# GpSimd's residual-and-bias sum and mask conversion wait for VectorE's second normalised rows

## The chip, the core and the metric

The kernel runs on one core of a Trainium2 chip. A core has TensorE (PE in the profile), VectorE (DVE), ScalarE (ACT), GpSimd (POOL) and SyncE (SP); each takes its own instructions in program order and meets the others only through semaphores. The metric is the time on the device in microseconds (us), as the median of several runs.

## What is computed

Two layers over `x` of shape (16, 256, 256): 16 entries of 256 tokens by 256 features. The first layer (conditioned normalisation, a router, eight experts) takes about the first 630 us and is not touched. The second is a transformer layer, cut here to what matters:

```python
x = _ln(src) * (1.0 + scale) + shift
q = (x @ Wq + bq); k = (x @ Wk + bk); v = (x @ Wv + bv)       # 16 heads of 16
scores = q @ k.T / 4 + attention_bias                          # (16, 16, 256, 256)
scores = where(src_mask, -inf, scores)
ctx = softmax(scores) @ v
x = x + (ctx @ Wo + bo)                                        # first residual
h = _ln(x) * g2 + beta2                                        # second normalisation
ff = _gelu2(h @ W1 + b1) @ W2 + b2
return x + ff                                                  # second residual
```

## The kernel before

**Staging.** `step(n, par)` is written once for each engine and called for n = -2 to 17. Step n holds the attention of entry n, and beside it the projections of entry n+1 and the end of entry n-1 (output projection, second normalisation, feed-forward). n = 3 to 12 are a hardware loop, two steps to a turn; the rest are unrolled. Within a step, PE, DVE and ACT go through 16 heads h and take up the other entries' work at fixed heads, so the order on each engine is written by hand. "An entry" below is one such step.

**Attention of one head.** PE `scores` (L1349, L1351) fills a PSUM bank from the mask and from q and k; DVE `minimum` (L1586, a custom instruction and an accumulator read for each of two halves) adds the bias and takes the row minimum; ACT `exponentials` (L1254) writes the probabilities over the bias; PE `turn_probs` (L1363) transposes them; ACT or DVE `take_probT` (L1260, L1592) brings them back to SBUF; PE `weigh` (L1379) multiplies by the values. `scores` and `turn_probs` alternate between two banks each, so PE's scores of head h+2 wait for the minimum of head h.

**The end of entry n-1, in step n.** DVE at h = 4: `residual` (L1633) writes `x3`, the first residual, and `moments` (L1639 to L1645) its mean and variance. GpSimd: `rsqrt` (L1180) turns the variance into `rstd2`. DVE at h = 5: `normalise2` writes the normalised rows `h_rows`, two instructions (one for each 128 tokens) of 128 x 256 float32, each with a mean and an inverse deviation per partition, each adding 1 to `h_rows_ready`:

```python
for j in range(J):
    dve.tensor_scalar(h_rows[:, j, :], x3[:, j, :], mv2[:, j, 0:1], rstd2[:, j:j + 1],
                      ALU.subtract, ALU.mult).then_inc(sem("h_rows_ready"), 1)
```

Right behind it DVE has `take_values` for entry n+1 (L1624, `v_pad`), the minimum of head 7 and `split_hT` (L1656). PE at h = 6 transposes `h_rows` (`turn_h`, L1448), ACT at h = 6 rounds the result (`take_hT`, L1289, `hT_hi`) and PE at h = 7 starts the feed-forward (`feed_up`, L1463). In the profile's tile names trailing numbers are cut, so `x3` is written x, `rstd2` rstd, `mv2` mv.

**GpSimd in step n.** Its queue holds: the gather for entry n+2 (L1185 to L1191); `rsqrt` of entry n-1; `prepare_sum` of entry n-1 (L1210: `x3b` = `x3` + `b2`, 128 x 512 float32, which only `finish` at h = 15 reads); `take_mask` of entry n+1 (L1205: the mask bytes become float32, first read by PE's scores at h = 14); four `lower_gelu` (L1198, `act_lo`); `rsqrt` of entry n+2.

**The xn rows.** `normalise` (L1576) at h = 14 is the same instruction as `normalise2` on other tiles (`src` to `xn`). `combine_second` (L1558) adds gathered rows to `src`, with both of its tensor inputs in SBUF.

Of the kernel before, what the change touches and what calls it, by code (L numbers as in the profile page):

```python
# [18 lines left out]
J = T // P  # L19
# [42 lines left out]
def wait_alone(eng, sem, value):  # L62


    if isinstance(value, int):
        eng.wait_ge(sem, value)
    else:
        value = eng.to_reg(value)
        eng.wait_ge(sem, 1)
        eng.wait_ge(sem, value)  # L70


def wait_free(eng, sem, value, alone=False):

    if isinstance(value, int):
        if value > 0:
            eng.wait_ge(sem, value)
    elif alone:
        wait_alone(eng, sem, value)
    else:  # L80
        eng.wait_ge(sem, value)


def exists(n):

    return not isinstance(n, int) or 0 <= n < B
# [8 lines left out]
def entries(eng, step):  # L95


    for n in range(-2, 3):
        step(n, n % 2)
    with eng.Fori(1, B // 2 - 2) as i:  # L100
        step(2 * i + 1, 1)
        step(2 * i + 2, 0)
    for n in range(B - 3, B + 2):
        step(n, n % 2)


def spread(ap, shape, at):

    return ap.unsqueeze(at).to_broadcast(shape)
# [874 lines left out]
def transformer(nc, ctx, io, keep):  # L984
# [3 lines left out]
    def sem(name):  # L988
        if name not in sems:
            sems[name] = ctx.enter_context(nc.semaphore(name))  # L990
        return sems[name]
# [181 lines left out]
    @block.gpsimd  # L1173
    def _(pool):
        pool.memset(minus_half[:], -0.5).then_inc(sem("half_set2"), 1)
        pool.wait_ge(sem("half_set2"), 1)

        def rsqrt(out, var, ready, done, n):
            pool.wait_ge(sem(ready), n + 1)
            pool.tensor_tensor(out[:], var[:, :, 1], minus_half[:], ALU.pow).then_inc(sem(done), 1)  # L1180

        def gather(n):
            wait_free(pool, sem("src_read"), n)
            wait_free(pool, sem("xmT_ready"), C * n)
            pool.tensor_copy(gate_now[:], gates[:, bass.ds(n, 1), :, :].rearrange("p b k j -> p (b k j)")).then_inc(sem("entry_cols"), 1)  # L1185
            pool.tensor_copy(mod_now[:, 0, :], scale[:, :, bass.ds(n, 1)].rearrange("p c b -> p (c b)")).then_inc(sem("entry_cols"), 1)
            pool.tensor_copy(mod_now[:, 1, :], shift[:, :, bass.ds(n, 1)].rearrange("p c b -> p (c b)")).then_inc(sem("entry_cols"), 1)
            pool.tensor_copy(row_now[:], out_row[:, bass.ds(n, 1), :].rearrange("p b q -> p (b q)")).then_inc(sem("entry_cols"), 1)
            wait_alone(pool, sem("entry_cols"), 4 * (n + 1))
            for q in range(K * J):  # L1190
                pool.indirect_dma_start(picked_rows[:, q, :], None, io["expert_out"],  # L1191
                                        bass.IndirectOffsetOnAxis(ap=row_now[:, q:q + 1], axis=0),
                                        bounds_check=TILES * TOK - 1, oob_is_err=False).then_inc(sem("rows_in"), 16)

        def lower_gelu(n, pair):
            wait_alone(pool, sem("act_upper"), 4 * n + pair + 1)
            at = 2 * pair % 4
            pool.tensor_tensor(act_part["lo"][:, 2 * pair:2 * pair + 2, :], up_f[:, at:at + 2, :],  # L1198
                               act_part["hi"][:, 2 * pair:2 * pair + 2, :].bitcast(F32), ALU.subtract).then_inc(sem("act_split"), 1)

        def take_mask(n, par):
            wait_alone(pool, sem("mask_in"), 16 * (n + 1))
            if at_least(n, 2):
                wait_alone(pool, sem("scores_done"), H * (n - 1))
            pool.tensor_scalar(mask_f[par][:], mask[:].bitcast(U8), 1.0, None, ALU.mult).then_inc(sem("mask_taken"), 1)  # L1205

        def prepare_sum(n):
            pool.wait_ge(sem("x3_ready"), n + 1)
            wait_free(pool, sem("out_sent"), 16 * n)
            pool.tensor_tensor(x3b[:], x3[:], spread(b2[:], [P, J, D], 1), ALU.add).then_inc(sem("x3b_ready"), 1)  # L1210

        def step(n, par):
            if exists(n + 2):
                gather(n + 2)
            if exists(n - 1):
                rsqrt(rstd2, mv2, "var2_ready", "rstd2_ready", n - 1)
                prepare_sum(n - 1)
            if exists(n + 1):
                take_mask(n + 1, 1 - par)
            if exists(n - 1):  # L1220
                for pair in range(4):
                    lower_gelu(n - 1, pair)
            if exists(n + 2):
                rsqrt(rstd, mv, "var_ready", "rstd_ready", n + 2)

        entries(pool, step)

    @block.scalar
# [572 lines left out]
def at_least(n, least):  # L1801

    return not isinstance(n, int) or n >= least
# [88 lines left out]
```

## Time and profile before

| | |
|---|---|
| median of 3 runs | 1423.8 us (1423.69 to 1425.08) |
| the profiled execution: time, span | 1427.18 us, 1425.4 us |
| busy over the span: PE, DVE, ACT, POOL | 1276.8, 988.0, 903.1, 665.1 us |
| granted TensorE clock, mean | 0.976 of full speed |
| one entry of the transformer, steady part | about 46 us |

The span runs from the first to the last instruction of the profiled execution. Busy time of an engine is an average over stages with different limits; what a change does is read from the waits of the stage in which it lies.

### The profile page before, as it was taken

Reading aid. Unit: us, or ns where it says so; the run is one execution under the profiler, and the core shown is the slowest. Engines: PE = TensorE matmul, PEld = TensorE weight load, DVE = VectorE, ACT = ScalarE, POOL = GpSimd, SP = SyncE. Lnnn points to the kernel's source line nnn. Section 1 sums busy time; section 2 is a strip of 40 time slices with the busy share of each in tenths; the row PEclk is TensorE's granted clock in tenths of the full one; section 3 lists DMA queues with packets and bytes.
Section 4 is the critical chain, followed back from the end, with each engine's and each line's share of the span. In section 5 each row is a group of like instructions: output and inputs, shape, how many; then the busy total and the mean of one; then the engine's idle time right before and its main releaser. Section 6 shows DMA issues by size and latency. Waiting matters only on the chain. (4 is left out here: it accounts for less than half of the span.)

```text
span 1425.4 us, 34480 instructions
## 1 busy us (share of the span) xinstructions
PE 1276.8 (90%) x9923; PEld 1160.8 (81%) x9923; DVE 988.0 (69%) x2764; ACT 903.1 (63%) x2319; POOL 665.1 (47%) x580
## 2 busy tenths in 40 slices
PE   5884899999999999945899999999999999999996
PEld 4774899999999999944587888778877878788885
DVE  5776688889878987743776667566766667666652
ACT  3442677778777877722566676666666666667671
POOL 2775577787778777743032332332232232231221
PEclk9999999999999999976899999999999999999997
DMA  5885121121112111128766656655675556654620
GB/s 189 271 274 187 46 66 46 57 61 51 57 48 65 54 56 58 49 89 253 225 214 184 190 182 198 205 181 162 195 220 182 177 179 204 199 189 148 202 72 15
DMA packets 184707, 203.18 MB, mean 143 GB/s; under 512 B 18176, under 2 KB 172736, under 8 KB 184576
## 3 DMA queue, kind: packets, MB, share of 16 engines
q1 hardware_dynamic: 169136, 161.57, 36.9%
q10 hardware_dynamic: 9264, 23.47, 5.1%
q0 software_dynamic: 6176, 16.79, 3.4%
q14 instruction: 96, 0.79, 0.2%
q8 instruction: 35, 0.57, 0.2%
HBM read 155.89 MB, written 41.68 MB: 139 GB/s over the span
## 5 line engine op out<-in xcount | busy, mean ns | idle before, releaser
L1254 ACT ACTIVATE bias<-bias,neg_max 128x256 f32<-128x256 f32 x512 | 255.4, 501 | 193.7 <-DVE neg_max L1586 191.6
L343 POOL TENSOR_TENSOR w_lo<-w,w_hi 128x512 fp32r<-128x512 f32 x156 | 242.2, 1572 | 0.0
L1586 DVE CUSTOM_DVE_ANT_0 bias<-ps_s,bias 128x256 f32<-128x256 f32 x512 | 194.5, 417 | 34.0 <-PE ps_s L1351 21.4
L745 DVE TENSOR_TENSOR w_lo<-w,w_hi 128x512 fp32r<-128x512 f32 x156 | 149.8, 999 | 68.7 <-ACT w_hi L423 67.0
L544 PE MATMUL ps_y<-w_hi,hidT_hi 128*128 128x256 f32 x624 | 180.2, 289 | 1.9 <-DVE token_rows L759 1.9
L531 PE MATMUL ps_h<-htokT_hi,w_hi 128*128 128x256 f32 x624 | 178.5, 286 | 3.2 <-DVE htokT_lo L750 3.2
L531 PE MATMUL ps_h<-htokT_lo,w_hi 128*128 128x256 f32 x624 | 178.2, 286 | 0.0
L531 PE MATMUL ps_h<-htokT_hi,w_lo 128*128 128x256 f32 x624 | 178.1, 285 | 0.0
L1349 PE MATMUL ps_s<-mask_f,minus_ident 128*128 128x256 f32 x512 | 154.3, 323 | 25.6 <-DVE neg_max L1586 15.8
L544 PE MATMUL ps_y<-w_lo,hidT_hi 128*128 128x256 f32 x624 | 177.0, 284 | 0.0
L544 PE MATMUL ps_y<-w_hi,hidT_lo 128*128 128x256 f32 x624 | 177.0, 284 | 0.0
L1198 POOL TENSOR_TENSOR act_lo<-up_f,act_hi 128x512 fp32r<-128x512 f32 x64 | 82.6, 1291 | 198.1 <-ACT act_hi L1301 198.1
L1363 PE MATMUL ps_p<-const,bias 128*128 128x128 f32 x1024 | 158.7, 278 | 16.9 <-ACT bias L1254 15.6
L1349 PEld LDWEIGHTS ps_s<-mask_f,minus_ident 128*128 128x128 f32 x512 | 97.9, 191 | 59.1 <-DVE neg_max L1586 39.5
L1180 POOL TENSOR_TENSOR rstd<-mv,minus_half 128x2 f32<-128x2 f32 x32 | 23.2, 724 | 254.4 <-DVE mv L1645 179.9
L1363 PEld LDWEIGHTS ps_p<-const,bias 128*128 128x128 f32 x1024 | 116.6, 141 | 29.3 <-issue 17.9
L1351 PE MATMUL ps_s<-k_stack,q_stack 128*128 128x256 f32 x512 | 134.2, 284 | 0.0
L531 PEld LDWEIGHTS ps_h<-htokT_hi,w_hi 128*128 128x128 f32 x624 | 121.5, 195 | 3.9 <-DVE htokT_lo L750 3.9
L544 PEld LDWEIGHTS ps_y<-w_hi,hidT_hi 128*128 128x128 f32 x624 | 120.0, 192 | 2.1 <-DVE token_rows L759 2.1
L531 PEld LDWEIGHTS ps_h<-htokT_lo,w_hi 128*128 128x128 f32 x624 | 121.5, 195 | 0.0
L531 PEld LDWEIGHTS ps_h<-htokT_hi,w_lo 128*128 128x128 f32 x624 | 121.4, 195 | 0.0
L544 PEld LDWEIGHTS ps_y<-w_lo,hidT_hi 128*128 128x128 f32 x624 | 120.3, 193 | 0.0
(276 smaller groups left out, 3496.9 us busy)
## 6 DMA issues: line engine op xcount, KB each, us to landing
bias<-bias_dram SPq DMA_DIRECT2D x128, 512.0 KB, 4.2
w<-w_dram ACTq DMA_DIRECT2D x32, 512.0 KB
xin<-dispatch SPq DMA_DIRECT2D x39, 256.0 KB, 2.8
expert_out<-token_rows SPq DMA_DIRECT2D x39, 256.0 KB, 2.2
q_stack<-q_hi_rows SPq DMA_DIRECT2D x64, 128.0 KB, 2.9
q_stack<-q_lo_rows SPq DMA_DIRECT2D x64, 128.0 KB, 2.9
k_stack<-k_hi_rows SPq DMA_DIRECT2D x60, 128.0 KB, 2.8
k_stack<-k_lo_rows SPq DMA_DIRECT2D x60, 128.0 KB, 2.8
```

The costliest lines, as they stand in the source:

```text
L343: pool.tensor_tensor(w2_part["lo"][:, k, :], w2_piece(e, k), w2_part["hi"][:, k, :].bitcast(F32), ALU.subtract).then_inc(sem("w2_split"), 1)
L531: last = pe.matmul(ps_h[f // 2][:, (f % 2) * TOK:(f % 2 + 1) * TOK], w1_part[a][:, C * (f // 4) + c, (f % 4) * P:(f % 4 + 1) * P], htokT[b ...
L544: last = pe.matmul(ps_y[j][:, 0:D], hidT[a][:, f, j * P:(j + 1) * P], w2_part[b][:, k, (f % 2) * D:(f % 2 + 1) * D], start=(f == 0 and n = ...
L745: dve.tensor_tensor(w1_part["lo"][:, k, :], w1_piece(e, k), w1_part["hi"][:, k, :].bitcast(F32), ALU.subtract).then_inc(sem("w1_split"), 1)
L1180: pool.tensor_tensor(out[:], var[:, :, 1], minus_half[:], ALU.pow).then_inc(sem(done), 1)
L1198: pool.tensor_tensor(act_part["lo"][:, 2 * pair:2 * pair + 2, :], up_f[:, at:at + 2, :], act_part["hi"][:, 2 * pair:2 * pair + 2, :].bitca ...
L1254: act.activation(head_rows(h, j), head_rows(h, j), ACT.Exp, scale=-1.0, bias=neg_max[par][:, h, j:j + 1], accum_out=total[par][:, h, j:j + ...
L1349: pe.matmul(ps_s[h % 2][:, j * T:(j + 1) * T], minus_ident[:], mask_f[par][:, j, :], start=True, stop=False)
L1351: last = pe.matmul(ps_s[h % 2][:, j * T:(j + 1) * T], q_stack[par][:, h, j * P:(j + 1) * P].bitcast(F32R), k_stack[par][:, h // 2, :].bitc ...
L1363: last = pe.transpose(ps_p[h % 2][:, kt * T + j * P:kt * T + (j + 1) * P], head_rows(h, j)[:, kt * P:(kt + 1) * P], ident)
L1586: dve.tensor_tensor_reduce(head_rows(h, j), ps_s[h % 2][:, j * T:(j + 1) * T], head_rows(h, j), -1.0, LARGEST, ALU.add, ALU.min, neg_max[p ...
```

## The change

One wait is added on GpSimd, ahead of `prepare_sum`. `J` is 2 and `h_rows_ready` counts two per entry, so `J * n` is reached when both instructions of `normalise2` for entry n-1 have written. `take_mask` and all that follows stand behind it in the same queue.

```diff
             if exists(n - 1):
                 rsqrt(rstd2, mv2, "var2_ready", "rstd2_ready", n - 1)
+                pool.wait_ge(sem("h_rows_ready"), J * n)
                 prepare_sum(n - 1)
             if exists(n + 1):
                 take_mask(n + 1, 1 - par)
```

On GpSimd, in the even step of the hardware loop, the rows read as follows (`x3b<-x,b` is the sum, `mask_f<-mask` the conversion; REGISTER_ALU rows work out a semaphore's value):

```order
 L1179 REGISTER_ALU
 L1180 TENSOR_TENSOR rstd<-mv,minus_half 128x2 [waits var2_ready]
-L1210 TENSOR_TENSOR x3b<-x,b 128x512 [waits out_sent,x3_ready]
+L1217 REGISTER_ALU
+L1210 TENSOR_TENSOR x3b<-x,b 128x512 [waits out_sent,x3_ready,h_rows_ready]
 L68 REGISTER_ALU
 L68 REGISTER_ALU [waits mask_in]
```

No instruction changes its place; the sum gets one more semaphore to wait for, and a register instruction that works out `J * n`.

On DVE, at heads 5 to 6 of a step in the same loop, the rows are these before the change, and the same after it (the ISA rows of L1586 are the minimum of a head, `v_pad<-ps_q,bv` is `take_values`):

```order
L1586 ISA bias,neg_max<-ps_s,bias 128x256
L1586 ISA neg_max 128x1
L1651 TENSOR_SCALAR h_rows<-x,mv,rstd 128x256 [waits h_turned,rstd2_ready]
L1651 TENSOR_SCALAR h_rows<-x,mv,rstd 128x256
L1624 TENSOR_TENSOR v_pad<-ps_q,bv 128x4x4x16 [waits pv_done,v_done]
L1624 TENSOR_TENSOR v_pad<-ps_q,bv 128x4x4x16
L68 REGISTER_ALU
L1586 ISA bias,neg_max<-ps_s,bias 128x256 [waits scores_done]
L1586 ISA neg_max 128x1
```

Nothing moved here: the `h_rows` pair still waits for `rstd2` and still stands ahead of the values and of the minimum of head 7; what is new is that GpSimd's sum starts behind the pair instead of beside it.

## Rows read from the trace of the kernel before

**Rows 1.** One entry's stretch: length, busy us by engine, clock, DMA
```profile
core 0: us, PE busy (x) PEld busy (x) DVE busy (x) ACT busy (x) POOL busy (x), PEclk, DMA share, GB/s
754.00:799.70 45.70, 43.02 (x352) 36.99 (x352) 30.55 (x106) 30.33 (x94) 14.08 (x16) 1.00 0.63 193
```

**Rows 2.** Timeline, one entry, heads 4 to 8: start, length, engine, idle before
```profile
769.52 1.89 PE L1438 MATMUL ps_q<-wv,xmT 128*128 128x256 f32 x8
...
771.61 0.28 PE L1351 MATMUL ps_s<-k_stack,q_stack 128*128 128x256 f32 x1
...
773.06 1.27 POOL L1210 TENSOR_TENSOR x3b<-x,b 128x512 f32<-128x512 f32 x1
773.11 2.00 DVE L1651 TENSOR_SCALAR h_rows<-x,mv,rstd 128x256 f32<-128x256 f32 x2
...
774.17 0.65 PE L1363 MATMUL ps_p<-const,bias 128*128 128x128 f32 x4 [0.17 <-ACT bias L1254]
774.32 1.53 POOL L1205 TENSOR_SCALAR mask_f<-mask 128x512 fp32r<-128x512 uint8 x1
...
775.03 0.74 DVE L1624 TENSOR_TENSOR v_pad<-ps_q,bv 128x256 f32<-128x256 f32 x2
...
775.16 0.66 PE L1448 MATMUL ps_k<-const,h_rows 128*128 128x128 f32 x4 [0.34 <-DVE h_rows L1651]
...
776.49 0.51 ACT L1254 ACTIVATE bias<-bias,neg_max 128x256 f32<-128x256 f32 x1 [1.89 <-DVE neg_max L1586]
...
776.51 0.39 PE L1349 MATMUL ps_s<-mask_f,minus_ident 128*128 128x256 f32 x1 [0.69 <-DVE neg_max L1586]
...
777.63 0.66 PE L1363 MATMUL ps_p<-const,bias 128*128 128x128 f32 x4 [0.38 <-ACT bias L1254]
777.96 0.58 ACT L1289 ACTIVATE hT_hi<-ps_k 128x512 fp32r<-128x512 f32 x1
...
778.58 0.69 DVE L1656 SCALAR_TENSOR_TENSOR hT_lo<-ps_k,hT_hi 128x512 fp32r<-128x512 f32 x1 [2.12 <-ACT hT_hi L1289]
...
778.60 0.38 PE L1463 MATMUL ps_q<-hT_hi,ff_hi 128*128 128x256 f32 x1 [0.31 <-ACT hT_hi L1289]
```

**Rows 3.** Timeline of DVE: TENSOR_SCALAR from SBUF to SBUF with GpSimd idle
```profile
682.19 0.60 DVE L1685 TENSOR_SCALAR h_rows<-const,vec 128x128 f32<-128x128 f32 x2
...
796.83 0.74 DVE L1576 TENSOR_SCALAR xn<-src,mv,rstd 128x256 f32<-128x256 f32 x2 [0.16 <-POOL rstd L1180]
```

**Rows 4.** Timeline: DVE beside GpSimd's act_lo, and (698.23) with GpSimd idle
```profile
698.23 0.88 DVE L1552 SCALAR_TENSOR_TENSOR src<-picked_rows,gate_now,x 128x256 f32<-128x256 f32 x2
...
783.86 1.29 POOL L1198 TENSOR_TENSOR act_lo<-up_f,act_hi 128x512 fp32r<-128x512 f32 x1 [8.02 <-ACT act_hi L1301]
...
784.77 0.68 DVE L1664 SCALAR_TENSOR_TENSOR up_f<-tanh_f,ps_k 128x512 f32<-128x512 f32 x1
...
792.18 1.29 POOL L1198 TENSOR_TENSOR act_lo<-up_f,act_hi 128x512 fp32r<-128x512 f32 x1 [1.17 <-ACT act_hi L1301]
792.31 1.85 DVE L1558 SCALAR_TENSOR_TENSOR src<-picked_rows,gate_now,src 128x256 f32<-128x256 f32 x2
```

**Rows 5.** Instructions of L1586: duration ns min/median/max, first and last start
```profile
L1586 DVE CUSTOM_DVE_ANT_0 bias<-ps_s,bias x512: 401/418/426, 665.1 to 1385.2; 128x256 f32<-128x256 f32 x171
```

**Rows 6.** Timeline: the pair in the last two entries
```profile
1364.63 1.68 DVE L1651 TENSOR_SCALAR h_rows<-x,mv,rstd 128x256 f32<-128x256 f32 x2
...
1403.24 1.67 DVE L1651 TENSOR_SCALAR h_rows<-x,mv,rstd 128x256 f32<-128x256 f32 x2 [0.82 <-POOL rstd L1180]
```

**Rows 7.** Timeline of a loop entry: SP's bias load, DVE's minimum of head 14
```profile
923.01 1.10 SPq L1106 DMA_DIRECT2D bias<-bias_dram  x2
...
932.17 0.41 DVE L1586 CUSTOM_DVE_ANT_0 bias<-ps_s,bias 128x256 f32<-128x256 f32 x1
```

**Rows 8.** DMA issues of 891 to 940 us: KB each, median us to landing
```profile
bias<-bias_dram SPq DMA_DIRECT2D x9, 512.0 KB, 3.9
```

**Rows 9.** Timeline: PE's first scores of the next entry
```profile
797.06 0.39 PE L1349 MATMUL ps_s<-mask_f,minus_ident 128*128 128x256 f32 x1
```

## The prediction

> **What bounds the kernel now.** The change touches only the transformer, so I began with the busy table by stretches. In the steady part an entry takes 45.7 us, of which PE is busy 43.0, DVE and ACT 30 to 31, at full granted clock and with the DMA engines busy 0.63 of the time [rows 1]. PE sets the pace but stands still 2.7 us per entry, and only a change that removes part of this shortens an entry. The timeline of one entry shows where: around heads 6 and 7, PE waits 0.34 us for `h_rows`, 0.69 for a minimum, 0.38 for exponentials and 0.31 for `hT_hi`, 1.72 us in a row [rows 2]. All four follow from one lateness on DVE. Its two `h_rows` instructions start at 773.11 and take 2.00 us; then come, without a gap, the values and the minimum of head 7, whose end releases both ACT, at 776.49, after a wait of 1.89 us, and PE's next scores; and on ACT the exponentials of head 7 stand ahead of `hT_hi`, which releases DVE's `hT_lo` (waited 2.12 us) and PE's feed-forward [rows 2].
>
> The pair need not take 2.00 us. The same instruction on `xn`, same shape and same kind of scalars, takes 0.74 us for two with GpSimd idle [rows 3]. What differs is that GpSimd's sum starts 0.05 us ahead of the pair and runs 1.27 us, and the mask conversion follows at 774.32 [rows 2]. Two independent rows bear out that DVE is held there: a pair of scalar-tensor-tensor instructions with both tensors in SBUF takes 0.88 us with GpSimd idle and 1.85 when GpSimd's `act_lo` starts 0.13 us ahead of it [rows 4]; and in the last two entries, where the pair has the sum beside it but no mask conversion, it takes 1.68 and 1.67 us [rows 6].
>
> **What the change does, part by part.** GpSimd's sum now starts when both `h_rows` instructions have written.
>
> *The pair on DVE.* It starts as before, since `rstd2` comes before the wait. With nothing beside it I take 0.74 us, by the `xn` row. It saves 2.00 - 0.74 = 1.26 us in the entry shown; the other 13 entries with a mask conversion read 1.97 to 2.00, mostly 1.99, so 1.25 each. In the last two, 1.68 - 0.74 and 1.67 - 0.74, 0.94 and 0.93.
>
> *How much of it reaches the end of the entry.* DVE: the values were multiplied by 769.52 + 1.89 = 771.41 and the scores of head 7 were done at 771.89, so values and minimum follow at once and ACT is released at 775.23, not 776.49; it had waited 1.89 us, more than 1.26, so its exponentials come the full 1.26 earlier. PE: the transposition of `h_rows` can start only when the head before is done, at 774.82, so it ends at 775.48 (775.82 before, 0.34 gained). The scores then start at 775.48, 1.03 earlier, and end by about 776.2; the next transposition waits for ACT, at 777.63 - 1.26 = 776.37, so these scores are hidden. `hT_hi` starts on ACT at 776.70, when the transposed rows have lain there 1.2 us, and PE's feed-forward at 777.34 instead of 778.60. DVE's `hT_lo` waited 2.12 us and moves with it [rows 2]. From there all four engines stand 1.26 us earlier, and I count the whole of it.
>
> *What doesn't move with them.* SP's transfers start from earlier work. The nearest: the bias of heads 14 and 15 is issued at 923.01 [rows 7], lands in 3.9 us [rows 8], 926.9, and is read at 932.17 [rows 7]. That leaves 5.3 us, after the change about 4.0, so it costs nothing.
>
> *The two GpSimd instructions.* Sum and conversion start about 0.8 us later (773.85 for 773.06) and end near 776.7. Behind them in the queue stand `act_lo`, which waited 8.02 us [rows 4] and keeps over 6 of that, and, on SP, the next mask load, a step away. The mask is first read at 797.06 [rows 9], `x3b` only at the end of the step. All cost nothing; were the cover gone, the price would be the 0.8 us. The register instruction and the wait lie in the same idle time.
>
> *What the sum now lies beside.* This the trace does not show: 1.27 us of sum beside DVE's values and the minimum of head 7, both with PSUM as one input. Bounds: at best nothing (the values already take 0.74 us beside the conversion [rows 2], so there is hardly anything to gain either); at worst what `act_lo` did to the pair with two SBUF tensors, 1.85 - 0.88 = 0.97 us. I take nothing: the nearest rows are `up_f` (one SBUF input, one PSUM input), 0.68 us and begun while `act_lo` ran [rows 4], and the minimum, which over 512 runs never took more than 426 ns against a median of 418 [rows 5].
>
> The Trainium skill says on this case, in "SBUF — State Buffer", section "Who interferes with whom", that a VectorE instruction with at most one SBUF input outside the two-port modes does not contend with GpSimd; that would make the cost nothing too, for the sum as for the conversion.
>
> *Weighed against a rule.* The conversion beside the second `h_rows` instruction seems to cost little: the pair is 0.32 us longer with it than without (2.00 against 1.68) [rows 2, 6]. The same section of the Trainium skill says that between a two-port VectorE instruction and GpSimd whoever comes second is blocked until the other has finished. For the first instruction the trace agrees, since the pair cannot have ended before the sum did. For the second it does not: held for the whole conversion, to 774.32 + 1.53 = 775.85, the pair would have taken 3.0 us and more, and the row has 2.00. By that rule a saving reckoned from it would be some 2.3 us an entry, 35 in all; the measured length decides, and it gives 1.25.
>
> **Sum.** 14 x 1.25 + 0.94 + 0.93 = 19.4 us. The profiled execution had a span of 1425.4 and a time of 1427.2; the span becomes 1406.0. The median of the runs shown is 1423.8, 3.4 below that execution's time; less the same 19.4 it is 1404.4.
>
> **The rivals.**
> *1. Part of it is absorbed.* If after the transposition something other than DVE set PE's pace, each entry would give only PE's wait for `h_rows`, 0.34 us [rows 2], in the last entry all 0.93: 15 x 0.34 + 0.93 = 6.0 us, 1417.8. For it: PE is the busiest engine, and its scores at 775.48 gain only 1.03. Against: every later wait in the row names DVE or ACT work behind the pair. Chance 0.07, anywhere between.
>
> *2. No change, because `h_rows` is not slowed by GpSimd.* The price is then nothing, 1423.8. That would follow if the instruction used one SBUF input at one element a cycle. A row speaks against it: two of 128 x 128 take 0.60 us and two of 128 x 256 take 0.74 [rows 3], 0.14 us for 256 elements, while from PSUM 256 elements more cost 0.68 - 0.42 = 0.26 us [rows 4, 5]. The instruction runs at the double rate. Nor does anything but GpSimd explain 0.74 against 2.00. The case that the wait does nothing, because its count is reached too early, belongs here; the count is two per entry, so it does not. Chance 0.05.
> The Trainium skill ("SBUF — State Buffer", "Who interferes with whom") counts `tensor_scalar` in that double rate among those that contend, so it sides with the forecast.
>
> *3. Slower, because the hold moves.* Sum and conversion, 1.27 + 1.53 = 2.80 us from 773.85, now lie beside the values, the minimum of head 7 and the start of the chain to `hT_hi`. If DVE were held for all of it, an entry would lose 2.80 - 1.26 = 1.54 us; over 14 entries 21.6 us longer, 1445, less what the last two give. It decides from 1.26 us of stretch per entry. Against: the values beside the conversion are already seen unslowed, and so are `up_f` and the minimum. Chance 0.04, with smaller stretches in the forecast's range.
>
> **How the numbers follow.** The forecast has 0.84, and its own range is 1402 to 1409: below, a little more than the sum if runs scatter as before; above, 0.3 us per entry lost at PE or beside the sum. To hold 8 in 10 with the upper half of that and some of rival 1, I give 1402 to 1411. A measurement of this kernel tells about 0.2%, 2.8 us, from no change. Faster: the forecast and nearly all of rival 1, 0.90. Within 0.2%: rival 2 and the weakest end of rival 1, 0.06. Slower: 0.04.
>
> **What would show it.** In the changed kernel's timeline `h_rows` x2 reads 0.74 us in all 16 entries and GpSimd's sum starts as it ends. `v_pad` x2 stays at 0.74 and the minimum under 0.43. PE's waits at the transposition and the scores behind it nearly vanish, and an entry takes 44.4 to 44.7 us with PE still busy 43.0. The pair still near 2 us would show rival 2; the pair at 0.74 with `v_pad` or the minimum stretched, rival 3; all of these as forecast and an entry still above 45.1 us, rival 1, and then the wait that has grown names the cause. The forecast also fails if SP's transfers come late: DVE's minimum would then wait for a bias DMA.

## The result, and the profile after

| | before | after |
|---|---|---|
| median | 1424.44 us (4 runs, 1423.69 to 1425.38) | 1401.63 us (4 runs, 1397.94 to 1403.61) |
| ratio, 95% interval | | 0.9837 [0.9817, 0.9857] |
| profiled execution: time, span | 1427.18, 1425.4 us | 1400.47, 1398.7 us |
| granted TensorE clock, mean | 0.976 | 0.978 |

The kernel is 22.8 us faster. The forecast was 19.4 us, from 1423.8 (the median of three of the four runs before) to 1404.4, with a range from 1402.0: the result lies 2.8 us below the forecast and 0.4 below the range. The direction, the place and the mechanism came as written; the size is short, and most of what follows is about the 3.4 us by which the gain exceeds 19.4.

The timeline of the changed kernel at the same heads of the same entry, which answers to [rows 2] (`...` stands for lines left out):

```profile
768.99 0.74 DVE L1652 TENSOR_SCALAR h_rows<-x,mv,rstd 128x256 f32<-128x256 f32 x2
...
769.64 0.75 DVE L1625 TENSOR_TENSOR v_pad<-ps_q,bv 128x256 f32<-128x256 f32 x2
769.80 1.28 POOL L1210 TENSOR_TENSOR x3b<-x,b 128x512 f32<-128x512 f32 x1 [0.85 <-DVE h_rows L1652]
...
770.05 0.66 PE L1364 MATMUL ps_p<-const,bias 128*128 128x128 f32 x4 [0.18 <-ACT bias L1255]
...
770.54 0.60 PE L1449 MATMUL ps_k<-const,h_rows 128*128 128x128 f32 x4
...
771.05 1.50 POOL L1205 TENSOR_SCALAR mask_f<-mask 128x512 fp32r<-128x512 uint8 x1
771.11 0.51 ACT L1255 ACTIVATE bias<-bias,neg_max 128x256 f32<-128x256 f32 x1 [0.63 <-DVE neg_max L1587]
771.13 0.39 PE L1350 MATMUL ps_s<-mask_f,minus_ident 128*128 128x256 f32 x1
...
772.25 0.66 PE L1364 MATMUL ps_p<-const,bias 128*128 128x128 f32 x4 [0.38 <-ACT bias L1255]
772.58 0.58 ACT L1290 ACTIVATE hT_hi<-ps_k 128x512 fp32r<-128x512 f32 x1
...
773.20 0.69 DVE L1657 SCALAR_TENSOR_TENSOR hT_lo<-ps_k,hT_hi 128x512 fp32r<-128x512 f32 x1 [2.12 <-ACT hT_hi L1290]
773.22 0.39 PE L1464 MATMUL ps_q<-hT_hi,ff_hi 128*128 128x256 f32 x1 [0.31 <-ACT hT_hi L1290]
```

The pair takes 0.74 us for 2.00, the sum now names `h_rows` as what it waited for, `v_pad` keeps its length beside the sum, and PE's waits of 0.34 and 0.69 are gone while those of 0.38 and 0.31 stay. From the start of the pair to `hT_lo` it is 773.20 - 768.99 = 4.21 us, and in [rows 2] 778.58 - 773.11 = 5.47: the forecast's 1.26 us, to the hundredth.

All 32 instructions of the pair, the sum, and the minimum (duration in ns, min/median/max), the last for [rows 5]:

```profile
L1652 DVE TENSOR_SCALAR h_rows<-x,mv,rstd x32: 407/411/415, 725.3 to 1377.8; 128x256 f32<-128x256 f32 x32
L1210 POOL TENSOR_TENSOR x3b<-x,b x16: 1263/1278/1281, 726.1 to 1378.3; 128x512 f32<-128x512 f32 x16
L1587 DVE CUSTOM_DVE_ANT_0 bias<-ps_s,bias x512: 402/419/426, 664.6 to 1360.3; 128x256 f32<-128x256 f32 x171
```

The steady part by windows. Its first row is the entry of [rows 1], the second the 14 entries from the first `h_rows` pair to the 15th, the third the rest of the span:

```profile
core 0: us, PE busy (x) PEld busy (x) DVE busy (x) ACT busy (x) POOL busy (x), PEclk, DMA share, GB/s
749.70:793.60 43.90, 42.88 (x354) 37.23 (x353) 29.49 (x107) 30.40 (x94) 14.07 (x16) 1.00 0.63 200
725.30:1340.72 615.42, 591.75 (x4878) 513.01 (x4873) 405.85 (x1469) 422.54 (x1283) 186.98 (x207) 1.00 0.62 195
1340.72:1398.70 57.98, 46.21 (x350) 40.81 (x350) 22.22 (x69) 24.54 (x67) 13.59 (x11) 0.90 0.09 28
```

The same two stretches of the profile before, and PE's waits in ten entries of each kernel (us in total, times, longest), before first:

```profile
727.44:1364.63 637.19, 597.16 (x4881) 512.76 (x4873) 423.36 (x1469) 423.27 (x1283) 186.89 (x208) 1.00 0.61 188
1364.63:1425.40 60.77, 47.66 (x350) 41.64 (x350) 24.10 (x69) 24.57 (x67) 13.46 (x11) 0.88 0.08 27
```

```profile
PE ps_p L1363 <- ACT bias L1254: 10.1, 30, 0.4
PE ps_s L1349 <- DVE neg_max L1586: 7.8, 10, 0.8
PE ps_out L1420 <- DVE ctxT L1611: 4.6, 9, 0.5
```

```profile
PE ps_p L1364 <- ACT bias L1255: 10.3, 32, 0.4
PE ps_q L1464 <- ACT hT_hi L1290: 2.4, 10, 0.3
PE ps_out L1421 <- DVE ctxT L1612: 2.1, 4, 0.5
```

The 14 entries give 637.19 - 615.42 = 21.8 us, where the pair accounts for 14 x 1.25 = 17.5; the rest of the span behind them gives 2.8, for 1.87. Ahead of the first pair, where the change can do nothing, since the new wait first holds back the sum that used to lie beside that pair, it is 727.44 - 725.30 = 2.1 us. PE's wait for the minimum, 7.8 us, has left the list, which is the change. Its wait for `ctxT` (the result of the attention, transposed for the output projection) has halved too, though nothing near it was touched. These differences ask whether the profile before was typical.

### The profile page after: what moved, and what is told of

Same layout as the page of the kernel before. It is cut to its first block and busy times, and to the rows that moved or that the text cites. A ratio compares the mean times of both kernels' runs of the same rounds, so it can differ in the third digit from the quotient of the medians.

```text
span 1398.7 us, 34496 instructions
## 1 busy us (share of the span) xinstructions
PE 1266.9 (91%) x9923; PEld 1157.5 (83%) x9923; DVE 968.6 (69%) x2764; ACT 902.8 (65%) x2319; POOL 665.3 (48%) x580
```

## The experiments

Eleven runs on three chips of this kind; each set of repeats has its own runs of the kernel before on the same chip, and gains are reckoned from those.

**1. Both kernels again (e1, e2).** No edit.

> The kernel before, unchanged, run again. The hold on the h_rows pair must be there in the same size: 1.97 to 2.00 us in 14 entries, 1.67 and 1.68 in the last two. It is run for the surplus of the change over the forecast, which in the two profiles lies between finish and the ctxT product of the next step (heads 0 to 2): ACT starts the copy of head 2 late by 0.36 to 0.62 us in 9 entries of the kernel before, in none of the first 14 of the changed one. If that is a property of this kernel's timing, it shows here again in the same entries. If it belongs to one execution, it is gone or in other entries. Time: 1423 to 1427 us, ratio 1.000 in either case.

> The changed kernel, run again with more rounds, to size the gain. If the forecast's sum of 19.4 us was the whole of it and the rest was scatter of single executions (the four runs so far lie 5.7 us apart), the ratio is 0.9864 or nearer to 1. If the late copy of head 2 on ACT, 0.5 us in 8 or 9 entries, is really gone as well, 19.4 + 4.5 = 23.9 us go and the ratio is 0.983. The pair stays at 0.74 us, v_pad x2 at 0.74 to 0.75.

Measured: before 1425.0 us (1423.36 to 1426.97, 12 runs) and 1424.16 (17 more); after 1401.68 (1398.36 to 1402.91, 5 runs), ratio 0.9834 [0.9817, 0.985]. A gain of 22.5 us on this chip shows that the surplus over 19.4 isn't chance. In the profile of e1 PE's waits over the 14 entries, and under it the same row of e11 (below), the same kernel on another chip:

```profile
PE ps_out L1420 <- DVE ctxT L1611: 3.0, 5, 0.8
```

```profile
PE ps_out L1420 <- DVE ctxT L1611: 6.1, 13, 0.8
```

The wait for `ctxT` differs for one and the same kernel. Over all profiles the step on VectorE from `q_lo` (the low part of the projected queries) to `ctxT` reads 3.54 us in e1 to e4, 3.96 to 4.47 in eight of the entries of e5 to e8, and 3.8 to 4.2 in the same ones of e9 to e11, whichever kernel ran: among these three chips it goes by the chip. The profile before has 4.02 to 4.28 there, the one after 3.53 to 3.54, so 4.5 us of the 26.7 between their spans is no effect of the change. Nor are the 2.1 us ahead of the first pair: over the 13 profiles that pair starts at 725.3 to 729.6 us, whichever kernel ran. That leaves 20.1 us between the two profiles, for 19.4. The ratio of e2 is the one that its expectation gave for the late copy gone as well, but not for that reason, since on this chip the step is 3.54 us in both kernels. Why the medians differ by 22.5, and the two dips of the clock that e1 shows besides, come under 6.

**2. The conversion beside the pair (e3).**

```diff
                 rsqrt(rstd2, mv2, "var2_ready", "rstd2_ready", n - 1)
-                pool.wait_ge(sem("h_rows_ready"), J * n)
-                prepare_sum(n - 1)
             if exists(n + 1):
                 take_mask(n + 1, 1 - par)
+            if exists(n - 1):
+                pool.wait_ge(sem("h_rows_ready"), J * n)
+                prepare_sum(n - 1)
```

> GpSimd converts the mask right after the reciprocal root, beside the h_rows pair, and takes the sum only when the pair has written. If every GpSimd instruction holds the pair for its whole length, the first h_rows row waits for the conversion's end and the pair takes 1.53 + 0.70 = 2.2 us in 14 entries, so that all of the gain there is gone and a little more (14 x 0.2 = 3 us slower than before). If the conversion, which read only bytes and cost the second row 0.32 us, holds less, the pair takes 1.1 to 1.5 us and about half of the gain stays (10 us faster than before). In the last two entries there is no conversion and the pair takes 0.74 us in either case.

Measured: 1405.63 us (4 runs, 1405.57 to 1406.96), ratio 0.9872 [0.9855, 0.989], 3.95 above e2. One entry, and all instructions of the pair:

```profile
772.67 1.54 POOL L1205 TENSOR_SCALAR mask_f<-mask 128x512 fp32r<-128x512 uint8 x1
772.70 1.04 DVE L1653 TENSOR_SCALAR h_rows<-x,mv,rstd 128x256 f32<-128x256 f32 x2
```

```profile
L1653 DVE TENSOR_SCALAR h_rows<-x,mv,rstd x32: 399/410/721, 728.7 to 1383.6; 128x256 f32<-128x256 f32 x32
```

A conversion that starts 0.03 us ahead and runs 1.54 costs the pair 0.30 us, all in its first instruction (0.72 for 0.41); the second runs beside it at full speed. 14 x 0.30 = 4.2 us, and 3.95 were measured. The pair of 1.04 us is shorter than in either case of the expectation (1.1 to 1.5, or 2.2).

**3. The sum far away (e4).** The wait stays, with the conversion behind it; the sum goes behind the second `act_lo`.

```diff
                 pool.wait_ge(sem("h_rows_ready"), J * n)
-                prepare_sum(n - 1)
...
                 for pair in range(4):
                     lower_gelu(n - 1, pair)
+                    if pair == 1:
+                        prepare_sum(n - 1)
```

> As the changed kernel, but the sum comes between the second and the third act_lo, where GpSimd was idle 2.25 us, and only the mask conversion follows the pair. Beside the values and the minimum of head 7 there is then the conversion instead of the sum. If the sum costs nothing there, as forecast, v_pad x2 and the minimum read the same as in the changed kernel and the time is the same within 0.2%. If the sum did stretch them, this kernel is faster than the changed one by 14 times the stretch. The sum in the gap meets only PSUM-fed work on DVE; should it push act_lo later, feed-forward waits and it is slower by up to 0.3 us per entry, 4.8 us.

Measured: 1403.14 us (4 runs, 1402.33 to 1404.38), ratio 0.9853 [0.9835, 0.987]; `v_pad` 0.75, the minimum 0.42, the pair to `hT_lo` 4.20 to 4.21, all as in the changed kernel. The sum beside `v_pad` and the minimum costs nothing: there was nothing to win back.

**4. What of GpSimd's work holds the pair (e6, e7).** In e6 the sum waits for the first row only. In e7, on the kernel before, the instruction beside the pair has one input; `b2` is left out.

```diff
-                pool.wait_ge(sem("h_rows_ready"), J * n)
+                pool.wait_ge(sem("h_rows_ready"), J * n - 1)
```

```diff
-            pool.wait_ge(sem("x3_ready"), n + 1)
-            wait_free(pool, sem("out_sent"), 16 * n)
-            pool.tensor_tensor(x3b[:], x3[:], spread(b2[:], [P, J, D], 1), ALU.add)
+            wait_alone(pool, sem("x3_ready"), n + 1)
+            wait_free(pool, sem("out_sent"), 16 * n, alone=True)
+            pool.tensor_scalar(x3b[:], x3[:], 1.0, None, ALU.mult)
```

> The changed kernel, but GpSimd waits for the first h_rows instruction only, so that the sum starts about 0.1 us after the second one has begun. Theory 1 (VectorE gives way whenever GpSimd's sum runs): the second instruction takes about as long as the sum, 1.27 us and a bit, the pair 0.41 + 1.38 = 1.8 us with only 0.2 us saved against before, and the time is 1424.2 - 14 x 0.2 = 1421. Theory 2 (whoever starts second waits): the second row has begun already and takes 0.41, the sum waits for it and reads 1.3 to 1.6 us; the pair is 0.74 to 0.8 and the time that of the changed kernel, 1401.7. A pair of 1.2 to 1.5 us (1411 to 1416) would be neither: both slowed while they overlap.

> The kernel before, but GpSimd's instruction beside the pair multiplies x3 by 1.0 instead of adding b2 to it (the bias b2 is left out of the computation): one float32 tensor read instead of two, same output, same place; its waits stand in instructions ahead of it. Theory 1 (it is the two float32 inputs that hold VectorE; the conversion with its one input costs the pair 0.30 us): the first row takes 0.4 to 0.7, the pair 1.0 to 1.4 us with both GpSimd instructions beside it, and the time is 1424.2 - 14 x 0.8 - 2 x 0.6 = 1411.8, between 1408 and 1416. Theory 2 (any float32 instruction of GpSimd between SBUF tiles holds it): first row 1.38, pair 1.7 to 2.0, time 1422 to 1425.

Measured: e6 1406.18 us (4 runs, 1405.12 to 1408.12), ratio 0.9855 [0.984, 0.987]; e7 1411.12 (4 runs, 1410.48 to 1412.37), ratio 0.9892 [0.9877, 0.9908]. The kernel before took 1426.01 on this chip, 1.8 more than the expectations reckoned with. For e7 the pair's lengths give 14 x 0.95 + 2 x 0.64 = 14.6 us, and 14.9 were measured. First e6, then e7:

```profile
862.14 0.74 DVE L1652 TENSOR_SCALAR h_rows<-x,mv,rstd 128x256 f32<-128x256 f32 x2
...
862.63 1.39 POOL L1210 TENSOR_TENSOR x3b<-x,b 128x512 f32<-128x512 f32 x1 [0.53 <-DVE h_rows L1652]
```

```profile
771.17 1.54 POOL L1210 TENSOR_SCALAR x3b<-x 128x512 f32<-128x512 f32 x1
771.21 1.04 DVE L1651 TENSOR_SCALAR h_rows<-x,mv,rstd 128x256 f32<-128x256 f32 x2
```

In e6 the second row had begun when the sum came: the row keeps its 0.41, and the sum reads 1.38 (median) for 1.28, though in the entry shown 0.25 us of the row were still to come. In the kernel before, the sum came 0.05 us ahead, and the first row took up to 1.38. The one that starts second is the one that loses. The Trainium skill says so in "SBUF — State Buffer", section "Who interferes with whom": "Issue order, not op shape, decides who blocks." Here the traces agree for the sum, in both orders. The same section of the Trainium skill says that the other is held for the whole instruction. The traces bear this out only for VectorE behind the sum: e7's float32 instruction with one input starts 0.04 us ahead, runs 1.54, and costs the pair 0.30, as the byte conversion did. So the GpSimd instruction with two tensor inputs holds VectorE through, and the two with one only at their start. Whether it is the second input or the kind of instruction (TENSOR_TENSOR or TENSOR_SCALAR) that decides, e7 doesn't tell, since it changed both. The 2.00 us of [rows 2] come apart as 0.74 + 0.97 for the sum + 0.30 for the start of the conversion.

**5. The other collision (e8).** The additions of gathered rows, which read 0.99 and 1.85 us beside `act_lo`, move on VectorE to head 3, before `k_lo`.

```diff
+                if exists(n + 2) and not (isinstance(n, int) and n == -1) and h == 3:
+                    combine_first(n + 2)
+                    combine_second(n + 2)
...
-                    if h == 11:
-                        combine_first(n + 2)
-                    if h == 12:
-                        combine_second(n + 2)
```

> The changed kernel, and beside it the two additions of gathered rows (combine_first, combine_second, entry n+2) are moved on VectorE from heads 11 and 12, where GpSimd's act_lo runs beside them (0.99 and 1.85 us), to head 3, where VectorE stands idle for 2.4 us and GpSimd too. Theory (the same hold, the same cure): the second pair takes 0.88 instead of 1.85, and VectorE is free earlier at heads 11 and 12. PE stands still there for some 0.5 us at most, so 0 to 0.5 us an entry, 0 to 8 in all: 1394 to 1402. Rival A: nothing waits for VectorE at heads 11 and 12, and the time is 1401.7 within 2. Rival B: the gathered rows have not landed at head 3, or the 1.8 us there make the minimum and the residual late: slower than the changed kernel, 1405 and more.

Measured: 1409.44 us (4 runs, 1408.85 to 1410.67), ratio 0.9881 [0.9865, 0.9896]. That is 3.3 above e6, which has the pair of the changed kernel and ran on the same chip. Both pairs read 0.88 at head 3, as expected, and VectorE is busy 14 us less over the 14 entries (391.4 for 405.7). Yet PE's wait for `ctxT` over ten entries rises from 5.2 to 6.8 us, which makes about 2.2 of the 3.3 over 14 entries; the rest was not traced. This is rival B of the expectation. At heads 11 and 12 the list of PE's waits has no entry that the shorter pair could have removed, and at head 3 the moved work stands in the way. Since the move has this price, e8 doesn't show by itself that the hold at heads 11 and 12 costs nothing; it shows that what their removal brought, if anything, was less than that price.

**6. Where the rest of the gain comes from (e5, e9, e10, e11).** In e5 and e10 the changed kernel gets VectorE work of its own ahead of the pair, into a spare tile, with GpSimd idle. The edit of e5 (in e10 eight of width `P`):

```diff
             wait_free(dve, sem("h_turned"), n)
+            for k in range(4):
+                wide = D if k == 0 else P
+                dve.tensor_scalar(spare[:, k, 0:wide], x3[:, k % J, 0:wide], mv2[:, k % J, 0:1], rstd2[:, k % J:k % J + 1],
+                                  ALU.subtract, ALU.mult)
             for j in range(J):
```

> The changed kernel, with four more VectorE instructions of the kind of h_rows put ahead of the pair (one of 128 x 256, three of 128 x 128, into a spare tile that nobody reads): by the rows of xn (0.74 for two of 256) and of L1685 (0.60 for two of 128) they last 0.37 + 3 x 0.30 = 1.27 us, so that the pair ends where it ended before the change, with GpSimd idle all the while. Theory: what an entry costs is how late the pair is, whoever makes it late. Then h_rows to hT_lo, counted from the first of these instructions, is 5.46 to 5.48 us again (4.21 in the changed kernel), and the time is 1401.7 + 16 x 1.27 = 1422.0, between 1420 and 1425. Rival A: GpSimd's hold cost PE something of its own beside the delay: the delay alone gives clearly less than 1420. Rival B: the gain beyond 19.4 us comes with the delay itself (the shorter waits of PE, and with them its granted clock): the time is that of the kernel before, 1424 to 1425, with half-speed stretches in the steady part again.

> The changed kernel once more, to size its gain on a third chip. In the runs so far the gain was 19.8 us where the granted clock of the kernel before was 0.977 or more in 16 of 17 runs (e6, which has the pair at 0.74 too), and 22.5 where it was 0.971 to 0.974 in 12 of 17. Theory: the moved work is worth 19.4 us, and what comes beyond goes by how much lower the clock of the kernel before is than that of this one: 0.3 to 1 us beyond for equal clocks, 3 us for a difference of 0.003. Rival: the gain beyond 19.4 has nothing to do with the clock and comes out between 22 and 23 whatever the two clocks are.

> The changed kernel with eight VectorE instructions of 128 x 128 of the kind of h_rows put ahead of the pair (e5 had four, which moved the pair by 1.10 us). At 0.27 us each they move it by 2.15 us, in 16 entries 34.4 us. Theory (each microsecond of lateness of the pair is passed on in full, and PE, which then stands still longer in a row, is granted half speed now and then in the steady part): the changed kernel of the same chip + 34.4 + 3 to 6, so 37 to 41 more than it, with stretches of half clock in more entries than in e5, where two were seen. Rival A: the lateness is passed on in full and the clock has no part in it: 34 to 35 more than the changed kernel. Rival B: with 2.15 us a next thing is late (SP's transfers) and the time rises by over 45.

> The kernel before once more, one look, on the same chip as e9 and e10, to see its stretches of half clock and its step from q_lo to ctxT (3.54 us in one execution of it, 4.06 to 4.28 in nine entries of another) beside theirs. Theory: that step goes by the chip and not by the kernel, so it reads alike in all three; stretches of half clock in the steady part appear here and in e10, none in e9.

Measured: e5 1426.81 us (12 runs) where the kernel before has 1426.01 (17 runs): ratio 1.0 [0.999, 1.0009]. e9 1404.88 (5 runs), ratio 0.984 [0.9819, 0.9861]. e10 1446.72 (5 runs), ratio 1.0129 [1.0108, 1.0151]. e11, one run, 1426.04.

One entry of e5:

```profile
773.55 1.18 DVE L1654 TENSOR_SCALAR spare<-x,mv,rstd 128x256 f32<-128x256 f32 x4
774.65 0.73 DVE L1657 TENSOR_SCALAR h_rows<-x,mv,rstd 128x256 f32<-128x256 f32 x2
778.85 0.69 DVE L1662 SCALAR_TENSOR_TENSOR hT_lo<-ps_k,hT_hi 128x512 fp32r<-128x512 f32 x1 [2.12 <-ACT hT_hi L1291]
```

From the start of the spare work to `hT_lo` it is 5.30 us, where the kernel before has 5.46 from the start of the pair. The spare work moves the pair by 1.10 us in e5 and by 2.06 in e10. In e5 that is 17.6 us over 16 entries, and the time stands 20.6 above e6 of the same chip; in e10 it is 33.0, and the time stands 41.8 above e9. So a late pair costs more than its lateness. The windows show what comes on top. Each stretch of 7.00 us ends 0.55 us after `hT_lo` starts, the next follows it: e10, then e1, then e11, then e9.

```profile
868.00:875.00 7.00, 4.19 (x32) 2.86 (x24) 4.88 (x19) 3.63 (x11) 2.87 (x3) 1.00 0.78 234
875.00:878.40 3.40, 3.40 (x17) 3.22 (x16) 2.10 (x10) 2.20 (x8) 0.00 (x0) 0.50 0.67 206
...
918.40:965.85 47.45, 44.05 (x350) 38.43 (x350) 31.57 (x115) 30.66 (x92) 14.04 (x16) 0.96 0.59 183
965.85:1013.97 48.12, 44.44 (x350) 38.45 (x350) 31.52 (x116) 30.53 (x92) 14.05 (x16) 0.96 0.58 181
```

```profile
1047.00:1054.00 7.00, 4.97 (x41) 3.26 (x40) 4.74 (x14) 3.63 (x11) 3.49 (x3) 1.00 0.80 252
1054.00:1057.40 3.40, 3.40 (x17) 3.22 (x17) 2.11 (x10) 2.19 (x8) 0.00 (x0) 0.50 0.66 201
```

```profile
1047.04:1054.04 7.00, 4.98 (x41) 3.27 (x40) 4.74 (x14) 3.63 (x11) 3.50 (x3) 1.00 0.81 248
1054.04:1057.44 3.40, 3.19 (x25) 2.80 (x25) 2.65 (x11) 2.54 (x9) 0.00 (x0) 1.00 0.66 202
```

```profile
859.20:866.20 7.00, 5.85 (x50) 4.33 (x49) 4.53 (x18) 4.63 (x15) 3.48 (x3) 1.00 0.89 277
866.20:869.60 3.40, 3.19 (x26) 2.80 (x25) 2.65 (x11) 2.54 (x9) 0.00 (x0) 1.00 0.67 208
```

The feed-forward behind the pair runs at half clock, 1.2 GHz for 2.4, in e10 in every entry of the steady part (each of the 14 has a mean clock of 0.93 to 0.96); in the entry shown PE had been busy 4.19 of the 7.00 us ahead of it. In the kernel before PE is busy 4.97 of them, and the clock falls in two of the 14 entries of e1 and in none of e11's, at the same busy time, nor in any of the first profile's. In e5 it falls in two. In the changed kernel (e9) PE is busy 5.85, and the clock falls nowhere in the steady part of the eight profiles that have the pair at 0.74 or 1.04 us without spare work (after, e2, e3, e4, e6, e7, e8, e9). A fall costs about 1.0 us: 17 matmuls fit where 25 do, and the two entries of e1 read 47.30 and 46.17 us from pair to pair, where their like without a fall read 46.3 and 45.2.

The clock also differs where the change plays no part. The span behind the 14 entries, in e2 and then in e3, two kernels that have the same instructions in the same order there:

```profile
1342.40:1401.14 58.74, 46.96 (x350) 40.87 (x350) 22.21 (x69) 24.42 (x67) 13.57 (x11) 0.87 0.09 27
1348.09:1403.87 55.78, 43.84 (x350) 38.42 (x350) 22.22 (x69) 24.42 (x67) 13.56 (x11) 0.97 0.09 29
```

The same 350 matmuls take PE 3.1 us less at the higher mean clock, and the stretch is 3.0 us shorter. Ahead of the first pair the profiles hold 44 to 55 us at half speed, more than in the rest of the span together in every one but e10, and neither kernel has the less of it throughout.

Over all repeats, with the half-speed time of a run as 2 x (1 - mean clock) x its time:

| chip of | kernel | runs | mean time | half-speed time |
|---|---|---|---|---|
| e1, e2 | before | 29 | 1424.3 | 75.5 us |
| | changed | 5 | 1401.0 | 62.8 |
| e5 to e8 | before | 17 | 1426.6 | 65.8 |
| | e5 | 12 | 1426.5 | 74.2 |
| | e6 | 4 | 1406.4 | 64.7 |
| e9 to e11 | before | 10 | 1427.3 | 70.2 |
| | changed | 5 | 1405.4 | 62.4 |
| | e10 | 5 | 1446.9 | 115.2 |

A straight line through the 49 runs of before and changed on the first and third chip (a constant for each chip, one for the kernel, a slope on the half-speed time) gives 20.6 us for the kernel (standard error 0.6) and 0.20 us per us at half speed (0.03). By it 12.7 x 0.20 = 2.5 us of the first chip's gain go with the clock, and 7.8 x 0.20 = 1.6 of the third's. On the second chip, where the half-speed times are level, the medians of before and e6 are 19.8 us apart. The rival of e9, 22 to 23 whatever the clocks, is met by e9's 22.5 but not by this; e9 alone, whose clocks differ by 0.0024, fits its theory as well. The fit can't say where in the span the half-speed time lies. The profiles place in the steady part four falls in four executions with the pair 1.10 to 1.25 us late (before, e1, e11, e5), about 1 us each execution.

Against what was on record: e5 came out as its rival B, the time of the kernel before, though its lateness sums to 17.6 us and that of the kernel before to 19.4; the 8.4 us more at half speed make 1.7 of this by the fit. e10 a little over the theory's 37 to 41, which leaves rival A, 34 to 35, out; e11 showed no fall of the clock in the steady part, which its theory had expected.

## Where the prediction was right, and the step that failed

- **What bounds the kernel**: right. e5 shows it: with VectorE made late by other means and GpSimd idle, the time is that of the kernel before within 1 us. Beside the lateness, the sum and the conversion cost nothing that can be seen at this resolution, some 2 us, by which the two latenesses differ.
- **The pair at 0.74 us**: right, 0.74 by the view of the changed kernel, with each instruction at 407 to 415 ns; rival 2 is out.
- **The whole of 1.25 us reaches the end of the entry**: right. The pair to `hT_lo` is 4.21 us in all 14 entries (5.44 to 5.47 before), and all from `hT_lo` to the next pair takes what it took, but for the step to `ctxT` that goes by the chip. Rival 1, part of it absorbed, is out.
- **PE's scores behind the transposition**: they start 2.14 us after the pair for 3.40 before, 1.26 us earlier and not 1.03: the transposition starts at 770.54, where the view has the matmuls before it end at 770.71, and takes 0.60 for 0.66. Since PE waits behind these scores for the exponentials either way (0.38), nothing hangs on it.
- **The sum beside `v_pad` and the minimum costs nothing**: right, shown by e4. Rival 3 is out.
- **SP, `act_lo`, the mask**: nothing of them came late; the first `act_lo` of a step still waits 5.93 us and more for its input (over 6 was forecast).
- **A rule weighed, full blocking for the second row**: the row was rightly preferred. e3 and e7 show why: the conversion, and an instruction like it on float32, hold VectorE for 0.30 us, not through.
- **The entry at 44.4 to 44.7 us**: it reads 43.90 in the profile after, and 44.38 in e9, on a chip with the longer step to `ctxT`. The window of [rows 1] held some 0.5 us of that step.

The step that failed is the end of the sum, "less the same 19.4 it is 1404.4", and with it the low end of the range, "a little more than the sum if runs scatter as before". It took the difference of the medians for the moved work alone and put everything else by which they can differ at nothing; and the low end of 1402.0 took the scatter of three runs of the kernel before, 1.4 us, for that of the changed kernel, whose four runs span 5.7. In its place the runs showed a gain of 22.5 us on two chips (e2, e9) and of 19.8 on the third (e6, which has the pair of the changed kernel): 0.4 to 3.1 us beyond the term.

The term of 19.4 us itself holds. Between profiles of one chip the 14 entries differ by 18.0 us (e11 less e9) and 19.5 (e1 less e2, with two falls of the clock of 1.0 each), for 17.5, and the span behind them by 2.0 and 1.9, for 1.87. The stretch ahead of the first pair, where the change can't act, differs by -1.9 us in the one and +2.1 in the other: single executions differ there by about 2 us, whatever the kernel.

What lies beyond the term is in part PE's clock, which the prediction read as full from one entry of one execution [rows 1]. With the pair late by 2.06 us a half-speed stretch follows in every entry, and e10 shows that it is the lateness that brings it. At 1.10 to 1.25 us it follows now and then, worth about 1 us an execution in four profiles, and with the pair early in none of eight profiles; so the removal of the lateness very likely removes these. The fit puts 2.5, 1.6 and, on the chip where the half-speed times are level, 0.2 us down to the clock, but doesn't show that the change caused the whole of it, for profiles of kernels with an early pair differ by up to 3 us through the clock alone. Of the 22.5 us on the chips of e2 and e9, then, 19.4 are the pair, some 2 go with the clock, and about 1.2 stay open, twice the standard error of the fit: whether they are scatter, or falls of the clock that a mean to three decimals hides (0.001 is 2.8 us at half speed), these runs don't tell.

## What to carry to other kernels

When VectorE takes longer than the same instruction elsewhere, look at what GpSimd started just ahead of it. A GpSimd sum of two SBUF tensors held it for its whole 1.27 us, and a wait so that it starts behind VectorE's critical pair cost nothing. Look first who waits for VectorE there: moving other held work out of reach of GpSimd made the kernel slower (e8). Read the time ahead of the first place where a change can act, in both profiles: here it differed by 2 us by itself. When pricing a stall of PE, read the granted clock behind it in several executions: a stall removed may return a little more than its length, and one added may cost more (2.06 us of lateness cost 41.8 / 16 = 2.6 an entry in e10).

## What the runs showed that was not expected

- What GpSimd instructions cost the pair doesn't go by their length: 0.97 us for a sum with two tensor inputs (1.27 us long), 0.30 for an instruction with one input (1.54 long), bytes or float32.
- The clock is granted unevenly for equal busy time: PE busy 4.97 and 4.98 of 7.00 us, then 0.50 in one execution and 1.00 in the other.
- One and the same kernel has a step of 3.54 us on one chip and about 4.0 on another (`q_lo` to `ctxT`, eight entries). At mean clocks of 0.977 and 0.978 the kernel before took 1420.4 to 1424.6 us on the first chip and 1424.8 to 1429.1 on the second. What makes the difference was not looked into.
